# Attention over a paged cache: scores of three of four heads in fp32r parts, and the new keys of four heads in one transpose and one block-diagonal matmul

## What is computed

```python
x = x + conv(attention(x, Wq, Wk, Wv, Wo, ..., block_table, cache_seqlens))
# attention, cut:
q = rope(rmsnorm(x @ Wq.T)); k = rope(rmsnorm(x @ Wk.T)); v = x @ Wv.T
L = 512                                   # 16 pages of 32 keys
kc = k_cache[block_table]; vc = v_cache[block_table]
k_all = concat([kc, k]); v_all = concat([vc, v])      # 544 keys
valid = concat([arange(L) < cache_seqlens, ones(32)])
scores = einsum('bqhd,bkhd->bhqk', q, k_all) * SCALE
probs = softmax(where(valid, scores, -1e30))
o = einsum('bhqk,bkhd->bqhd', probs, v_all) @ Wo.T
```

## Time and profile before

| | us |
|---|---|
| median of three runs | 1365.14 |
| lowest, highest | 1363.93, 1365.40 |
| the profiled execution | 1361.4 |
| its span, first to last instruction | 1359.7 |

### The profile page before, as it was taken

One profiled execution on the slowest core, in us unless ns is written; L12 is line 12 of the kernel. 1 busy time (PEld: TensorE's weight loads), 2 busy tenths in 40 slices (PEclk: granted clock), 3 DMA queues, 4 the chain that ended last, 5 costly groups with the idle time before them and its releaser, 6 DMA issues.

```text
span 1359.7 us, 27056 instructions
## 1 busy us (share of the span) xinstructions
PE 1295.4 (95%) x7570; PEld 1091.1 (80%) x7570; DVE 819.8 (60%) x1659; ACT 590.4 (43%) x1678; POOL 511.2 (38%) x557
## 2 busy tenths in 40 slices
PE   6999989999999998998989999899999999999998
PEld 4778879999999996765657788799999999978756
DVE  5976556666666666852248765566666666665412
ACT  4576544444444443331136766444444444444320
POOL 3343444434434424533033443444343343354320
PEclk9999989999999999998989999899999999999999
DMA  6232487898788725305123314888888887334300
GB/s 236 94 124 78 138 233 218 226 242 233 212 214 220 213 63 175 128 0 186 48 102 125 133 62 125 250 220 235 235 222 216 209 222 216 75 105 143 109 0 31
DMA packets 138116, 214.78 MB, mean 158 GB/s; under 512 B 25076, under 2 KB 107318, under 8 KB 132022
## 3 DMA queue, kind: packets, MB, share of 16 engines
q1 hardware_dynamic: 125574, 202.75, 51.8%
q10 hardware_dynamic: 11664, 9.05, 2.1%
q0 software_dynamic: 800, 2.10, 0.6%
HBM read 203.33 MB, written 10.49 MB: 157 GB/s over the span
## 4 chain that ended last, share of the span: by engine, by line
PE 84%; DVE 6%; DMA 3%; issue 3%; ACT 2%; SPq 2%; ACTq 0%; POOL 0%; DVEq 0%; POOLq 0%; PEldq 0%
PE PS L963 21%; PE PS L936 10%; PE PS L919 9%; PE PS L924 8%; PE PS L881 5%; PE PS L877 5%; PE PS L873 5%; PE PS L1004 3%; PE PS L995 3%; PE PS L1001 3%; PE PS L1053 2%; PE PS L852 2%; PE PS L1032 1%; SPq L424 1%; DMA kv<-k_new 1%
## 5 line engine op out<-in xcount | busy, mean ns | idle before, releaser
L963 PE MATMUL PS<-probT,kv 128*128 128x128 f32 x2560 | 327.7, 275 | 0.0
L963 PEld LDWEIGHTS PS<-probT,kv 128*128 128x128 f32 x2560 | 306.0, 192 | 0.2
L756 ACT ACTIVATE ring<-ring,smin 128x544 f32<-128x544 f32 x192 | 143.9, 749 | 292.8 <-DVE smin L1361 292.8
L535 POOL TENSOR_SCALAR ring<-ring,rinv 128x544 f32<-128x544 f32 x192 | 138.6, 722 | 270.6 <-DVE rinv L1371 266.2
L1361 DVE CUSTOM_DVE_ANT_0 ring<-PS,mask,rq 128x544 f32<-128x544 f32 x192 | 150.5, 784 | 129.6 <-PE PS L924 129.0
L505 POOL TENSOR_TENSOR ring_parts<-ring,kv_parts 128x512 fp32r<-128x512 f32 x96 | 128.0, 1339 | 230.3 <-ACT kv_parts L636 230.2
L1367 DVE COPY probT<-PS 128x640 f32<-128x640 f32 x256 | 209.9, 820 | 3.2 <-PE PS L936 3.2
L919 PE MATMUL PS<-kv,q_now 128*128 128x288 f32 x512 | 170.1, 414 | 4.0 <-DMA kv<-k_new 4.0
L924 PE MATMUL PS<-kv,q_now 128*128 128x256 f32 x512 | 154.9, 385 | 0.0
L936 PE MATMUL PS<-consts,ring 128*128 128x128 f32 x960 | 136.4, 273 | 2.0 <-DVE probT L1367 1.7
L936 PEld LDWEIGHTS PS<-consts,ring 128*128 128x128 f32 x960 | 116.4, 141 | 22.2 <-POOL ring L535 2.4
(11 more groups left out here) (193 smaller groups left out, 1924.2 us busy)
## 6 DMA issues: line engine op xcount, KB each, us to landing
kv<-in_kpages SPq DMA_DIRECT2D x512, 128.0 KB, 2.3
kv<-in_vpages SPq DMA_DIRECT2D x496, 128.0 KB, 3.4
ring<-in_w SPq DMA_DIRECT2D x46, 1024.0 KB, 4.9
kv<-in_xT SPq DMA_DIRECT2D x4, 1024.0 KB, 8.8
v_new<-kv ACTq DMA_DIRECT2D x16, 256.0 KB, 5.2
k_new<-kv ACTq DMA_DIRECT2D x16, 256.0 KB, 2.3
kv<-k_new SPq DMA_DIRECT2D x32, 128.0 KB, 2.8
kv<-v_new SPq DMA_DIRECT2D x32, 128.0 KB, 2.5
```

The source lines that it names most:

```text
L535: nc.gpsimd.tensor_scalar(a, a, rinv[:, g:g + 1], 1.0, ALU.mult, ALU.mult).then_inc(p_ready, 1)
L756: nc.scalar.activation(a, a, ACT.Exp, scale=-1.0, bias=smin[:, g:g + 1], accum_out=rsum[:, g:g + 1]).then_inc(exp_done, 1)
L963: mm = nc.tensor.matmul(PS[:, at:at + D], vbuf(bpar)[:, c, gg * D:(gg + 1) * D], probT[:, g % 2, c * P:(c + 1) * P], start=(c == 0), stop= ...
```

## The change

- **Scores.** For a = 0, 1, 2 of each quad, q and k are split into an fp32r upper part and the rest. ACT makes `q_hi` (384 columns, `upper_q`) and `k_hi` (544 columns per head, two buffers, `upper_keys`, issued two steps ahead as soon as the scores of the step before are done); DVE makes `q_lo` (`lower_q`, once per quad, behind the reciprocal of a = 1); POOL makes `k_lo` in place over the keys (`lower_keys`), ahead of its scaling of step g-2. PE then does three products, hi*hi, hi*lo, lo*hi, of 288 and 256 columns each. For a = 3 the fp32 matmuls stay. The keys of the next element are now waited for by ACT in step 6 of the element before.
- **New keys.** POOL scales the 32 new columns into `prob_new`, 32 x 4 heads side by side, and the 512 others in place. PE transposes four heads' new columns at once (`turn_new`); ACT copies the four 32-row strips into the diagonal of a zeroed 128 x 512 tile (`spread_new`); one fp32 matmul of 512 columns adds them to the whole bank (`values_new`). `turn_probs` and `values` have four blocks instead of five, and the copy to `probT` is 512 wide.
- **Layout of the new values.** `v_new` in memory is now (element, head in quad x token, 2 x 128). `store_v` issues four DMAs of 32 x 4 x 128 instead of one of 128 x 512.
- **Mask.** `iota` times 2^100, minus length times 2^100, and max with 0, as add/max instead of is_ge/mult. The zero fillings by POOL of the fifth value block go.
- `v_free` is given by the first score matmul of step 4.

```diff
-                    for c in range(5):
+                    for c in range(4):
                         mm = nc.tensor.transpose(PS[:, 2048 + c * P:2048 + (c + 1) * P],
                                                  prob(g % PRING)[:, c * P:(c + 1) * P], ident)
...
+                    mm = nc.tensor.matmul(PS[:, at:at + mid], q_hi[:, u, q], hi[:, 0:mid], start=True, stop=False)
+                    if g == GU and not first:
 
                         mm.then_inc(v_free, 1)
...
+                    nc.tensor.matmul(PS[:, at + mid:at + LK], q_hi[:, u, q], hi[:, mid:LK], start=True, stop=False)
+                    pe.wait_ge(klo_ready, (h * HB + b) * NSB + e + 1)
+                    nc.tensor.matmul(PS[:, at:at + mid], q_hi[:, u, q], lo[:, 0:SPLIT, g, :],
+                                     start=False, stop=False)
...
+                    pe.wait_ge(spread_ready, GU * (h * QUADS + b * UNITS + u + 1))
+                    nc.tensor.matmul(bank(6 + u), vnew(par)[:, u * D:(u + 1) * D], spread, start=False, stop=True)\
+                        .then_inc(o_done, 1)
...
+                        if g % GU < NS:
+                            e = g // GU * NS + g % GU
+                            pool.wait_ge(khi_ready, (h * HB + b) * NSB + e + 1)
+                            pool.sem_inc(pool_past, 1)
+                            nc.gpsimd.tensor_tensor(
+                                kbuf_lo(par)[:, :, g, :], kbuf(par)[:, :, g, :],
+                                k_hi[:, e % 2, :].rearrange("p (j t) -> p j t", t=PSIZE), ALU.subtract)\
+                                .then_inc(klo_ready, 1)
...
+                    if (g + 2) % GU < NS and not (last and g + 2 >= HK):
+
+                        act.wait_ge(s_ready, s + 1)
+                        if g + 2 < HK:
+                            upper_keys(b, par, g + 2)
+                        else:
+                            upper_keys(b + 1, 1 - par, g + 2 - HK)
...
+                    if g % GU == 1 and not (first and g < GU):
+                        spread_new(b if g > GU else b - 1, int(g < GU))
+                    if g % GU == 0 and not first:
+                        keep_o(b - 1, g // GU)
...
+                        if g % GU == 1:
+                            nb, u = (b, 1) if g == 1 else ((b + 1) % HB, 0)
+                            dve.wait_ge(qhi_ready, h * (QUADS + 1) + b * UNITS + g // GU + 2)
+                            dve.sem_inc(dve_past, 1)
+                            lower_q(u, ds(nb * (HQ * SEQ) + u * GU * D, NS * D))
...
+                    for n in range(4):
+                        act.dma_start(vn_d[ds(h * HB + 4 * m + n, 1), :, col * D:(col + 1) * D]
+                                      .rearrange("o (a t) d -> t (o a) d", a=GU),
+                                      stage[n * SEQ:(n + 1) * SEQ, m % 2, :].rearrange("t (a d) -> t a d", a=GU))\
+                            .then_inc(vn_out[m % 2], 16)
```

More of the change, by code:

```diff
@@ L21 @@
 LK = LC + SEQ
-PW = 5 * P
 PRING = 4
@@ L30 @@
 UNITS = HK // GU
+NS = GU - 1
+NSB = UNITS * NS
 SLOTS = 4
@@ L542, in mask_of, with lower_keys @@
                     pool.sem_inc(pool_past, 1)
-                    nc.gpsimd.tensor_scalar(mask[:, par, 0:LC], con("iota"), len_now[:, par:par + 1], BIG,
-                                            ALU.is_ge, ALU.mult).then_inc(mask_ready, 1)
-                def scale_batch(b, par, first, last=False):
+                    nc.gpsimd.tensor_scalar(mask[:, par, 0:LC], con("iota"), len_now[:, par:par + 1], 0.0,
+                                            ALU.add, ALU.max).then_inc(mask_ready, 1)
+                def lower_keys(b, par, first, last=False):
                     for g in range(HK):
                         s = h * STEPS + b * HK + g
-                        if not first or g >= 2:
-                            scale_probs(s - 2, (g - 2) % HK)
+                        if g % GU < NS:
[6 more added lines that the diff above has]
+                                .then_inc(klo_ready, 1)
+                        if g >= 2:
+                            scale_probs(b, g - 2, first)
+                        elif not first:
+                            scale_probs(b - 1, g - 2 + HK)
                         if g == 3 and not last:
@@ L917, in scores @@
+                    if a == 0:
+                        pe.wait_ge(qlo_ready, h * (QUADS + 1) + b * UNITS + u + 1)
+                    e = u * NS + a
+                    pe.wait_ge(khi_ready, (h * HB + b) * NSB + e + 1)
+                    hi, lo = k_hi[:, e % 2, :], kbuf_lo(par)
                     q = slice(a * D, (a + 1) * D)
[L919 to L920 removed]
@@ L921, in scores @@
-                    if g == 3 and not first:
+                    mm = nc.tensor.matmul(PS[:, at:at + mid], q_hi[:, u, q], hi[:, 0:mid], start=True, stop=False)
+                    if g == GU and not first:
                         mm.then_inc(v_free, 1)
-                    nc.tensor.matmul(PS[:, at + mid:at + LK], q_now[:, u, q], kbuf(par)[:, SPLIT:NPP + 1, g, :],
-                                     start=True, stop=True).then_inc(s_ready, 1)
+                    nc.tensor.matmul(PS[:, at + mid:at + LK], q_hi[:, u, q], hi[:, mid:LK], start=True, stop=False)
@@ L927, in turn_probs @@
+                    nc.tensor.matmul(PS[:, at + mid:at + LK], q_lo[:, u, q], hi[:, mid:LK],
+                                     start=False, stop=True).then_inc(s_ready, 1)
                 def turn_probs(b, g, first):
@@ L941, in turn_probs, with turn_new @@
                     mm.then_inc(pt_ready, 1)
+                def turn_new(b, u, first):
+                    pe.wait_ge(new_scaled, h * STEPS + b * HK + (u + 1) * GU)
+                    if not (first and u == 0):
+                        pe.wait_ge(spread_ready, GU * (h * QUADS + b * UNITS + u))
+                    nc.tensor.transpose(PS[:, 2560:2688], prob_new[:, u, :], ident).then_inc(new_turned, 1)
                 def values(b, par, g, first):
@@ L1123, in prologue @@
                 link(V.tensor_copy(lens_b[:, :], lens_bi[:, :]))
+                link(V.tensor_scalar(lens_b[:, :], lens_b[:, :], -BIG, BIG, ALU.mult, ALU.add))
                 link(V.memset(mask[:, :, LC:LK], 0.0))
```

210 lines of the change are left out of this document (123 added, 87 removed).

## The result

The changed kernel takes 1373.87 us (median of 6 runs, 1368.35 to 1375.55); the kernel before, on the same chip, 1365.17 us (6 runs, 1363.93 to 1368.53). The ratio is 1.0054 with a 95% interval of 1.0041 to 1.0066: it is slower by 0.54%, where 1337 us and a gain were forecast. The profiled execution of the changed kernel has a span of 1366.6 us against 1359.7 before, so 7 us are to be explained there.

What follows compares the result with a forecast made beforehand. TensorE was taken as the bound. Its work -55 us, +14 for VectorE's late copy, +3 loads, +7 and +3 seams gave -28 from 1361.4, 1333.4; with 3.7 for the median, 1337 us, range 1313 to 1374.

Steps and rivals of the forecast that it cites:

- POOL chain: GpSimd in attention: subtractions, scalings and a 0.7 us mask fill 16.3 of 18.9 us a batch; no cost.
- What bounds the kernel before: Attention: TensorE runs without gaps, 2.58 us a step, 20.65 a batch; only less TensorE work shortens a step.
- PE work of a quad: TensorE's scores, transposes and values for four steps: 10.32 to 9.46 us, minus 55 us over 32 batches.
- The DVE and ACT chain: Behind VectorE's q subtraction the copy to probT is late for TensorE: 0.22 us lost a quad, plus 14 in all.
- Rival 2: GpSimd's mask stays at 2.0 us, making subtractions and scalings behind it late: plus 32 us, 1369; chance 0.10.
- Rival 1: VectorE's q subtraction meets GpSimd's subtraction and takes 0.65 us more a quad: plus 42 us, 1379; chance 0.17.
- Rival 3: K and V page loads stay at their early cycle, about 20.1 us a batch, and set the pace: 1357; chance 0.12.
- Loads and seams: Late K loads plus 3 us, later first scores after the projection plus 7, start of halves plus 3.

Runs made afterwards that it cites:

- b_mask_act: Changed kernel with the same mask computed by ScalarE (Relu of iota plus bias) and no mask on GpSimd; 1332.90 us, ratio 0.9774.
- c_new_only: Changed kernel with all scores in fp32 as before, so no key or query copies and no subtractions; new keys' part kept; 1350.02 us, ratio 0.9893.
- a_mask_mult: Changed kernel with GpSimd's mask instruction as multiply/multiply instead of add/max, so mask values are wrong; 1334.28 us, ratio 0.9777.
- e_two_early: Changed kernel with two of four heads split instead of three and GpSimd's mask two heads earlier; 1337.40 us, ratio 0.9798.
- j_split_only: Kernel before, with three of four heads split for fp32r scores; new keys in a fifth block and mask in old form; 1369.33 us, ratio 1.0030.
- i_seam: b_mask_act with Exp's table loaded in the wait for v_new and the first mask behind the first two key copies; 1330.91 us, ratio 0.9738.
- k_stage: i_seam with the last two stores of v_new staged in the two mask buffers; 1330.74 us, ratio 0.9747.
- g_best: b_mask_act with v_new laid out for one DMA per store, Exp's table load earlier, first mask behind first key copies; 1337.59 us, ratio 0.9799.
- d_split_two: Changed kernel with two of four heads split instead of three, mask place unchanged; 1373.51 us, ratio 1.0069.

## Why the prediction was wrong

The step that failed is the POOL chain: the mask was priced at 0.7 us and its effect put at no cost. It took 2.0 us, stood ahead of the subtraction that TensorE needs next, and cost 42 us. The other terms together came out near their sum.

The span's difference can be put together from the same places in both profiles. Each number is a duration in us, from that kernel's own profile; attention is from the first scores to the first matmul of the output projection:

| stretch | before | after | `b_mask_act` |
|---|---|---|---|
| start to first scores, first half | 177.47 | 181.45 | 182.87 |
| attention, first half | 337.17 | 335.81 | 315.31 |
| its end to the first scores of the second half | 345.07 | 349.64 | 353.59 |
| attention, second half | 337.15 | 335.9 | 315.43 |
| rest | 162.8 | 163.8 | 162.7 |

Point by point, in the prediction's order:

- **What bounds the kernel before: right.** `c_new_only`, which takes work from TensorE and gives GpSimd little, got faster by just that work.
- **PE work of a quad: right.** Forecast 9.46, and 9.48 where no wait falls. Transposes and values came out exact (`c_new_only`, 19.93), and a split head saves 0.16 to 0.17 in three kernels (`b_mask_act`, `e_two_early`, `j_split_only`), where 0.17 was forecast: the six matmuls cost 0.76 and not 0.75. The block-diagonal matmul stands in the unsplit step (3.11 in `c_new_only`), not in a split one (the prediction's 2.95); the quad's sum is the same. In all -54 us, forecast -55.
- **The DVE and ACT chain, +14: the right wait at the right place, oversized.** VectorE's subtraction of q takes 0.56 as forecast, delays the copy to probT behind it, and the transposes behind the unsplit scores wait for that copy and start 0.15 after its end (0.14 forecast). The wait is there in ten quads of fourteen and at most 0.11, not 0.22 in each. From 9.48 to the mean of 9.57 it is 0.09 a quad, 6 us in all.
- **The POOL chain, "no cost": wrong, and this step turned the sign.** Its terms: subtraction 1.35 (forecast 1.35), main scaling 0.70 (0.69), new part 0.30 to 0.42 (0.15 to 0.19), mask 2.0 (0.7). The prediction had the row of the mask at 2.00 and the bounds 0.7 to 2.0, and took the low end because add/max "too is plain arithmetic". The row nearest in operation was the mask itself, a form with a comparison; max belongs with it. `a_mask_mult` prices this one choice at 40 us (1373.87 against 1334.28). The prediction itself gave the subtractions behind a mask a cover of only 0.3 us, and 1.3 more on GpSimd is beyond it.
- **Rival 2 (the mask stays at 2.0) is what happened.** Its mechanism was right, the subtractions in the quad behind the mask came late. It was sized at 1 us a batch and was 1.32 (20.47 - 19.15), so 42 us and not 32. Head 4's step is 1.14 us longer than in `b_mask_act` (3.55 against 2.41), the next one 0.17. It had a chance of 0.10 and deserved most of it.
- **Rival 1 (the q subtraction meets GpSimd): not on VectorE.** It stayed at 0.56. The other side paid: GpSimd's 128x32 scaling beside it takes 0.56 to 0.69 (mostly 0.67) instead of 0.29, once a quad; in `c_new_only`, which has no subtraction of q, all 256 take 0.29. The Trainium skill ("SBUF — State Buffer", SBUF: two separate sides) says that a VectorE operation with two SBUF inputs and a GpSimd one that reads SBUF exclude each other for a whole instruction; the trace agrees, with GpSimd as the one that waits, though its row begins first (393.88 against 393.92). In most quads this costs nothing: in `b_mask_act` the transposes start 0.65 or more after the scaling they need. But in the quad of the mask it stands in the unbroken row of GpSimd's work ahead of head 4's subtraction. By these rows (0.67 - 0.29) it makes up to 0.38 of the 1.32 us a batch, an estimate: no run has the mask at 2.0 us without the subtraction of q.
- **Rival 3 (loads set the pace): not here.** Neither TensorE nor ScalarE waited for a K or V page in the steady part of the changed kernel. In other versions they did: ScalarE waited for K in `e_two_early`, `i_seam` and `k_stage`, TensorE for V in `g_best`.
- **Loads and seams, +13: right in sum.** The profile has 4.0 before the first scores, 4.6 between the halves and 1.0 in the rest. Attention as a whole gained 1.4 and 1.25 where sixteen batches at 0.18 make 2.9 each, so 3.1 went at its two starts: 12.7 in all. The first scores at 181.45 were forecast at 181. The loads' 3 us did not come. In their place stands Exp's table load, which the prediction did not price: in the kernel before it lay in a wait of ScalarE, now it follows the third key copy and the first Exp waits for it.

```profile
184.27 0.66 ACT L784 ACTIVATE k_hi<-kv 128x544 fp32r<-128x544 f32 x1 [2.33 <-PE PS L997]
184.95 1.28 ACT L817 ACT_TABLE_LOAD   x1
```

The sum after the fact: -54 for TensorE's work, +6 for the copy, +42 for the mask, +13 for the seams make +7, the 7 us of the spans; forecast were -55, +14, nothing, and +13.

What stays open: the between-halves stretch is 4 us longer in `b_mask_act` than in the changed kernel. From the start of the output projection to the second half's projections it takes 182.1 us against 179.3, and in the first 5 us of that the granted clock is 0.70 against 1.00. The other kernels fall into the same two groups: with 1.00 there (the kernel before, `c_new_only`, `g_best`) the stretch takes 179.3 to 179.8, with 0.50 to 0.68 (the other seven) 181.1 to 183.2. What decides whether the clock falls there was not tested, nor where the remaining 1.2 us go. The third split head of each quad gained only 0.06 (`e_two_early`, 9.63, to `b_mask_act`, 9.57) instead of 0.16: the wait for the copy took the other 0.09 to 0.10, and the subtraction of q is 0.56 us there and 0.43 with two split heads. A kernel that moves only that subtraction was not run.

## What to carry to other kernels

Before work goes to an engine that looks half idle, write down its order around the one result that the critical engine takes next: `d_split_two` and `e_two_early` have the same instructions, and 36 us between them. Price a changed operation by the row that shares its slowest part (here the comparison), not by the one that shares its shape, and where a bound decides the sign, forecast from the bad end. A rival whose condition is a price already standing in the trace deserves the larger chance.
